# Attention with the keys on the partitions: row maximum from a separate pass, probabilities never transposed

## The reference, cut to what matters

```python
q = (x @ wq).reshape(B, S, 8, 64)      # S = 1250 tokens, 8 heads of 64
k = (x @ wk).reshape(B, S, n_kv, 64)   # repeated to 8 heads
v = (x @ wv).reshape(B, S, n_kv, 64)
scores = einsum('bhqd,bhkd->bhqk', q, k) / sqrt(64)
attn = softmax(scores, axis=-1)        # over the 1250 keys
out = einsum('bhqk,bhkd->bhqd', attn, v)
x = x + out.reshape(B, S, 512) @ wo
```

## Time and profile before

| | |
|---|---|
| median of 3 runs | 1988.69 us (1987.15 to 1989.66) |
| the profiled execution, span from first to last instruction | 1983.8 us |
| PE busy | 1641.4 us, 83% of the span, 7770 matmul instructions |
| PE weight loads busy | 1121.7 us |
| DVE, ACT, POOL busy | 798.2, 506.5, 391.0 us |
| chain that ended last | PE 58%, DMA 15%, DVE 13%, ACT 6% |

### The profile page before, as it was taken

One profiled execution on the slowest core, in us unless ns is written; L12 is line 12 of the kernel. 1 busy time (PEld: TensorE's weight loads), 2 busy tenths in 40 slices (PEclk: granted clock), 3 DMA queues, 4 the chain that ended last, 5 costly groups with the idle time before them and its releaser, 6 DMA issues.

```text
span 1983.8 us, 19802 instructions
## 1 busy us (share of the span) xinstructions
PE 1641.4 (83%) x7770; PEld 1121.7 (57%) x7770; DVE 798.2 (40%) x1511; ACT 506.5 (26%) x734; POOL 391.0 (20%) x248
## 2 busy tenths in 40 slices
PE   1999979989998849888888887899888751999895
PEld 1547645456555638677777763465765641656452
DVE  5021051399502652477777863360334224111100
ACT  1101102012301032477777751100214110101000
POOL 3100021020201120244444423200211002222112
PEclk9999999989998969899999998999998855999997
DMA  4000010100020010101000003000200452699993
GB/s 169 0 0 1 0 44 0 58 1 1 41 86 0 6 64 33 46 14 27 14 13 14 22 8 142 5 22 0 85 0 1 177 224 98 266 406 402 404 418 129
DMA packets 23236, 170.74 MB, mean 86 GB/s; under 512 B 4259, under 2 KB 4805, under 8 KB 16886
## 3 DMA queue, kind: packets, MB, share of 16 engines
q1 hardware_dynamic: 19568, 164.44, 21.0%
q0 software_dynamic: 3584, 5.12, 1.2%
HBM read 153.06 MB, written 16.49 MB: 85 GB/s over the span
## 4 chain that ended last, share of the span: by engine, by line
PE 58%; DMA 15%; DVE 13%; ACT 6%; issue 4%; POOL 2%; another core or an unknown queue 1%; SPq 0%; DVEq 0%; POOLq 0%; ACTq 0%
PE psum L839 15%; DMA out_x<-arena,idx 12%; PE psum L849 9%; PE psum L866 6%; PE psum L980 6%; PE psum L1065 4%; PE psum L858 4%; PE psum L1053 3%; DVE arena_r L1449 3%; PE psum L1035 2%; DMA xf_dram<-arena 2%; DVE neg_max L1428 2%; ACT arena_r L762 1%; DVE ln_st L1219 1%; DVE arena L1227 1%
## 5 line engine op out<-in xcount | busy, mean ns | idle before, releaser
L839 PE MATMUL psum<-arena 125*128 125x512 f32 (+3 forms) x864 | 306.5, 516 | 14.4 <-DMA arena<-in_w_in 11.6
L839 PEld LDWEIGHTS psum<-arena 125*128 125x128 f32 (+1 forms) x864 | 164.1, 190 | 156.2 <-issue 142.2
L866 PE MATMUL psum<-arena 128*125 128x512 f32 (+3 forms) x464 | 162.6, 509 | 17.1 <-DVE arena L1556 9.0
L541 POOL TENSOR_SCALAR arena<-arena,row_inv 125x1250 f32<-125x1250 f32 x40 | 138.4, 3459 | 192.3 <-DVE row_inv L1436 192.3
L1200 PE MATMUL psum<-arena 128*39 128x512 f32 (+1 forms) x704 | 159.1, 609 | 13.2 <-DMA arena<-in_w_down 10.2
L1053 PE MATMUL psum<-ident,arena 125*125 125x125 f32 x800 | 125.6, 283 | 49.8 <-DVE arena_r L1449 48.5
L1449 DVE TENSOR_TENSOR arena_r<-psum,arena_r 125x500 fp32r<-125x500 f32 x200 | 131.9, 672 | 42.1 <-ACT arena_r L762 32.3
L1053 PEld LDWEIGHTS psum<-ident,arena 125*125 125x125 f32 x800 | 102.9, 188 | 63.0 <-DVE arena_r L1449 58.3
L762 ACT ACTIVATE arena_r<-psum 125x500 fp32r<-125x500 f32 x200 | 114.3, 586 | 88.0 <-PE psum L1053 87.8
L866 PEld LDWEIGHTS psum<-arena 128*125 128x125 f32 (+2 forms) x464 | 81.2, 191 | 95.2 <-issue 71.4
L980 PE MATMUL psum<-arena 125*125 125x512 bf16 (+1 forms) x588 | 119.8, 359 | 12.8 <-DVE arena L1340 11.3
(11 more groups left out here) (279 smaller groups left out, 2051.4 us busy)
## 6 DMA issues: line engine op xcount, KB each, us to landing
arena<-in_w_down SPq DMA_DIRECT2D x32, 2816.0 KB, 23.5
arena<-in_w_up SPq DMA_DIRECT2D x32, 682.5 KB, 19.4
a_spill<-arena SPq DMA_DIRECT2D x1, 6103.5 KB
arena<-a_spill SPq DMA_DIRECT2D x1, 6103.5 KB
bc<-k_dram SPq DMA_DIRECT2D x16, 312.5 KB, 4.2
gw<-in_gw SPq DMA_DIRECT2D x2, 2048.0 KB, 10.6
arena<-in_wkqv SPq DMA_DIRECT2D x1, 3072.0 KB, 16.4
arena<-in_x SPq DMA_DIRECT2D x10, 250.0 KB
```

What stands on the lines that cost most here:

```text
L541: pool.tensor_scalar(PR[i], PR[i], row_inv[:, i:i + 1], None, ALU.mult).then_inc(p_even, 1)
L839: ins = pe.matmul(o[0:w, lo:hi], lhs(c, m), rhs(c)[:, lo:hi], start=c == 0, stop=c == k - 1)
L866: ins = pe.matmul(o[0:p, 0:w], lhs(c, t), rhs(c, t), start=c == 0, stop=c == k - 1)
```

## The change

K is projected before Q. For each head, PE first makes the whole 1250 x 1250 score matrix from the high parts alone, 64 rows deep, queries on the partitions, one tile of 125 queries at a time (`max_scores`, one PSUM region); DVE takes the negated row maximum of each tile. Ten matmuls with one stationary column each turn the ten columns of maxima into one row (`turn_max`), which ACT copies to row 64 of `QM`, below the high queries that a DMA copies there.

Then the scores are made again with the keys on the partitions. A step is one tile of 125 keys by 420 queries; a round is 10 steps, a head 3 rounds (`ROUNDS`, queries 0 to 420, 416 to 836, 830 to 1250), so 240 steps in all. `score_tile` sums two fp32r matmuls: high keys against high and low queries (128 rows), low keys and a row of ones against high queries and the row of negated maxima (65 rows). ACT writes the exponential to a ring of 6 tiles. `weigh_values` multiplies it by V in fp32, columns 0 to 210 to PSUM partitions 0 to 63, columns 210 to 420 to partitions 64 to 127. DVE adds the even tiles of a round, POOL the odd ones, and `key_sums` sums over the partitions with a stationary of ones (64 columns); DVE inverts and multiplies. The transposes, the parts of the probabilities, the scaling by the inverse and the parts of V are gone. The next head's 10 tiles of maxima are put into steps 0, 2, 5, 7, ... 22 of a head, its `turn_max` after step 25.

```diff
+QW, QH = 420, 210
+ROUNDS = [(0, QW), (416, 416 + QW), (N - QW, N)]
+STEPS = len(ROUNDS) * TILES
+MAX_STEPS = {0: 0, 2: 1, 5: 2, 7: 3, 10: 4, 12: 5, 15: 6, 17: 7, 20: 8, 22: 9}
+P_RING = 6
+        max_bank = psum[0:TOK, 0:1536]
+        mrow_bank = psum[0:1, 0:TILES * 128].rearrange("p (t n) -> p t n", n=128)
+        av_bank = [psum[:, 1536 + 512 * i:1536 + 512 * i + QH] for i in range(2)]
+        sum_bank = psum[:, 2560:2560 + QH]
+        st_bank = [psum[0:TOK, 3072 + 512 * i:3072 + 512 * i + QW] for i in range(2)]
...
 # SP, for each head h, after the two loads of KD
+                sp.wait_ge(q_hi, h + 1)
+                if h:
+                    sp.wait_ge(st_full, STEPS * (h - 1) + 1)
+                load("qm", QM[h % 2][0:DK].bitcast(F32), QS[64 * (h % 2):64 * (h % 2) + 64, h].bitcast(F32))
...
 # POOL
+                pool.tensor_tensor(KLO[h % 2][0:DK], KD[0:DK], KHH[h % 3][0:DK].bitcast(F32),
+                                   ALU.subtract).then_inc(k_split, 1)
...
+            for s in range(HEADS * STEPS):
...
+                elif t % 2 and t > 3:
+                    pool.wait_ge(p_ready, s + 1)
+                    pool.wait_ge(pool_added, adds_done(s) - 1)
+                    pool.tensor_tensor(SUM_POOL[rnd % 2], SUM_POOL[rnd % 2], PT[s % P_RING], ALU.add).then_inc(pool_added, 1)
+                if at == 4 and h + 1 < HEADS:
+                    split_keys(h + 1)
...
 # ACT
+            def max_row(h):
+                act.wait_ge(mrow_full, h + 1)
...
+                act.activation(row.rearrange("p (t n) -> p t n", n=TOK), mrow_bank[:, :, 0:TOK], ACT.Copy).then_inc(mrow_ready, 1)
+            for s in range(HEADS * STEPS):
+                h, at = divmod(s, STEPS)
+                act.wait_ge(st_full, s + 1)
+                if s >= P_RING:
+                    act.wait_ge(av_step, s - P_RING + 1)
+                    act.wait_ge((dve_added, pool_added)[(s - P_RING) % TILES % 2], adds_done(s - P_RING))
+                act.activation(PT[s % P_RING], st_bank[s % 2], ACT.Exp).then_inc(p_ready, 1)
+                if at == 12 and h + 2 < HEADS:
+                    key_highs(h + 2)
+                if at == 26 and h + 1 < HEADS:
+                    max_row(h + 1)
...
 # PE
+            def max_scores(h, t):
...
+                else:
+                    pe.wait_ge(max_ready, i)
+                for lo, hi in CHUNKS:
+                    ins = pe.matmul(max_bank[:, lo:hi], QS[own, h, tok(t)], KHH[h % 3][own, lo:hi], start=True, stop=True)
+                ins.then_inc(max_full, 1)
+            def score_tile(s):
...
+                if s >= 2:
+                    pe.wait_ge(p_ready, s - 1)
+                pe.matmul(o, KHH[h % 3][:, tok(t)], QS[:, h, q0:q1], start=True, stop=False)
+                pe.matmul(o, KLO[h % 2][:, tok(t)], QM[h % 2][:, q0:q1], start=False, stop=True).then_inc(st_full, 1)
+            def weigh_values(s):
...
+                pe.wait_ge(p_ready, s + 1)
+                for j in range(2):
+                    ins = pe.matmul(av_bank[rnd % 2][64 * j:64 * j + 64], VA[:, t, h * DK:h * DK + DK],
+                                    PT[s % P_RING][:, j * QH:j * QH + QH], start=t == 0, stop=t == TILES - 1)
+                ins.then_inc(av_step, 1)
+            def key_sums(rnd):
...
+                for i, sums in enumerate((SUM_DVE, SUM_POOL)):
+                    for j in range(2):
+                        ins = pe.matmul(sum_bank[64 * j:64 * j + 64], ones_dk[:], sums[rnd % 2][:, j * QH:j * QH + QH],
+                                        start=i == 0, stop=i == 1)
             for t in range(TILES):
                 split_row(ROW["ffn_v"] + t, t, XLT_PARTS, WV_PARTS)
+                if t < 7:
+                    max_scores(0, t)
+                elif t < TILES - 1:
+                    max_scores(0, t) if t == 7 else None
+                    max_scores(0, t + 1)
+            turn_max(0)
...
+            for s in range(HEADS * STEPS):
+                h, at = divmod(s, STEPS)
+                if s + 2 < HEADS * STEPS:
+                    score_tile(s + 2)
+                weigh_values(s)
+                if s % TILES == 3 and s >= TILES:
+                    key_sums(s // TILES - 1)
+                if h + 1 < HEADS:
+                    if at in MAX_STEPS:
+                        max_scores(h + 1, MAX_STEPS[at])
+                    if at == 25:
+                        turn_max(h + 1)
...
 # DVE
+            def normalise_heads(rnd):
...
+                dve.reciprocal(sum_inv[:], sum_bank).then_inc(sum_inverted, 1)
...
+                for j in range(2):
+                    half = slice(64 * j, 64 * j + 64)
+                    dve.tensor_tensor(ATT[own, h // 2, q0 + j * QH:q0 + j * QH + QH], av_bank[rnd % 2][half], sum_inv[half],
+                                      ALU.mult).then_inc(att_ready, 1)
+            for s in range(HEADS * STEPS):
...
+                elif t % 2 == 0 and t > 2:
...
+                    dve.tensor_tensor(SUM_DVE[rnd % 2], SUM_DVE[rnd % 2], PT[s % P_RING], ALU.add).then_inc(dve_added, 1)
+                if h + 1 < HEADS and at in MAX_STEPS:
+                    bound(h + 1, MAX_STEPS[at])
+                if t == 5 and rnd:
+                    normalise_heads(rnd - 1)
```

More of the change, by code:

```diff
@@ L228, in build @@
         KD = bc[:, 0:N]
[L229 to L235, removed]
+        KHH = [part_r(8, C * D, N), part_r(8, C * D + N, N), part_r(4, 0, N)]
+        KLO = [part_r(3, i * N, N, DK + 1) for i in range(2)]
+        QM = [part_r(3, (2 + i) * N, N, DK + 1) for i in range(2)]
+        VA = rows(7)
+        PT = [part(1, i * QW, QW, TOK) for i in range(P_RING)]
+        SUM_DVE = [part(1, (P_RING + i) * QW, QW, TOK) for i in range(2)]
+        SUM_POOL = [part(1, (P_RING + 2 + i) * QW, QW, TOK) for i in range(2)]
+        ATT = cols(2)
+        max_bank = psum[0:TOK, 0:1536]
[3 more added lines that the diff above has]
+        st_bank = [psum[0:TOK, 3072 + 512 * i:3072 + 512 * i + QW] for i in range(2)]
         XN2, XN2T = rows(1), cols(2)
@@ L708, in _, with key_highs @@
                 act.activation(XLT_PARTS[0][:, c], XLT[:, c], ACT.Copy).then_inc(xl_hi, 1)
+            act.wait_ge(loads["wk"], 16)
+            act.activation(WK_PARTS[0], WK, ACT.Copy).then_inc(proj_hi, 1)
             act.wait_ge(loads["wq"], 16)
             act.activation(WQ_PARTS[0], WQ, ACT.Copy).then_inc(proj_hi, 1)
-            act.wait_ge(loads["wk"], 16)
-            act.activation(WK_PARTS[0], WK, ACT.Copy).then_inc(proj_hi, 1)
+            drain_cols("ffn_k", 4, lambda m: KF[:, m])
+            act.wait_ge(loads["wv"], 16)
+            act.activation(WV_PARTS[0], WV, ACT.Copy).then_inc(proj_hi, 1)
+            def key_highs(h):
+                act.wait_ge(loads["kd"], 32 * (h + 1))
+                if h >= 3:
+                    act.wait_ge(st_full, STEPS * (h - 2))
+                act.activation(KHH[h % 3], KD, ACT.Copy).then_inc(k_hi, 1)
             for m in range(4):
@@ L745, in scale_odd @@
[L745 to L770 removed]
+                    act.wait_ge(st_full, STEPS * (h - 1))
@@ new lines, in max_row @@
+                row = QM[h % 2][DK:DK + 1]
+                act.activation(row.rearrange("p (t n) -> p t n", n=TOK), mrow_bank[:, :, 0:TOK], ACT.Copy).then_inc(mrow_ready, 1)
+            max_row(0)
+            act.wait_ge(rows_full, ROW["ffn_v"] + TILES)
+            key_highs(1)
+            for s in range(HEADS * STEPS):
[9 more added lines that the diff above has]
+                    max_row(h + 1)
@@ new lines, in turn_max @@
+            def turn_max(h):
+                pe.wait_ge(max_ready, TILES * (h + 1))
+                for t in range(TILES):
+                    ins = pe.matmul(mrow_bank[:, t, 0:126],
+                                    neg_max[:, TILES * (h % 2) + t:TILES * (h % 2) + t + 1], ident_r[:], start=True, stop=True)
+                ins.then_inc(mrow_full, 1)
+            def score_tile(s):
+                h, at = divmod(s, STEPS)
+                rnd, t = divmod(at, TILES)
+                q0, q1 = ROUNDS[rnd]
+                o = st_bank[s % 2]
+                if at == 0:
+                    pe.wait_ge(k_split, h + 1)
+                    pe.wait_ge(loads["qm"], 16 * (h + 1))
+                    pe.wait_ge(mrow_ready, h + 1)
+                if s >= 2:
+                    pe.wait_ge(p_ready, s - 1)
+                pe.matmul(o, KHH[h % 3][:, tok(t)], QS[:, h, q0:q1], start=True, stop=False)
+                pe.matmul(o, KLO[h % 2][:, tok(t)], QM[h % 2][:, q0:q1], start=False, stop=True).then_inc(st_full, 1)
@@ L1466, in _ @@
+            normalise_heads(HEADS * len(ROUNDS) - 1)
             for g, (lo, hi) in enumerate(GROUPS):
```

244 lines of the change are left out of this document (96 added, 148 removed), and 2 rows, old and new, of the table loads.

## The result

| | median us | range, runs | ratio to before |
|---|---|---|---|
| before | 1988.21 | 1987.15 to 1989.66 | |
| changed | 2009.48 | 1998.34 to 2015.26, 4 runs | 1.0098 [1.0064, 1.0132] |

The change makes the kernel slower by about 1%. I had forecast 1985.5 us, with 0.38 on slower and a range to 2022; the likeliest case was wrong. The profiled execution is the fastest of the four (1998.34 us, span 1996.5), 12.7 us longer than the one of before.

The account below looks back on a forecast made before the run. PE bounds, each change of array shape paid: the stage sums 45.6 + 1 + 7 x 44.9 + 34.4 + 3.2 = 398.5, taken as 395 against 398.2; 1980.6 span plus 4.9 gives 1985.5 us, range 1925 to 2022.

Parts of the forecast that it names:

- Prices on PE: Attention on PE: matmul prices per column and instruction, giving a 1.12 us step and 44.9 us per head.
- the stall: Near each head's end, PE stands 0.8 us behind ACT's copy of the row of maxima and the next exponential.
- Rival B: Value products: the two column halves don't overlap in a group of four; 42 us more, 2028 us; chance 0.10.
- 3.5 us off the stage: Tiles of maxima: half of 7 us taken off in case their 64-row loads come close together, giving 395.
- The change of shape: PE in every step: each change of array shape costs 0.093 us, plus the first load bare.
- Rival A: Attention steps: changing shape costs little, DVE binds at 36.4 us per head; about 70 us less, 1915; chance 0.20.
- DVE, ACT, POOL beside PE: Attention: the other engines stay off the path; per head ACT 20.5, DVE 28.3, POOL 16.3 of 44.9 us.
- rival C: Attention: DVE or POOL late, or ACT behind its key copy; 16 to 24 us more, 2002 to 2010; chance 0.20.
- The start: From V's projection to the first exponential: V ends at 828.0, first exponential at 833.4; 45.6 us plus 1 for the clock.
- then key_highs(1) 1.24: Before the first exponential: ACT's copy of head 1's high keys costs 1.24 us after the row of maxima.
- step 12: Within a head: ACT's high-key copy falls behind a tile of maxima, and its DMA has 8 steps to land.
- PE idles 3 us there and the clock may fall as it does now: Before the first exponential: PE idles 3 us, and a fall of the clock costs 1 us.

Follow-up runs that it names:

- e8: e5 with ScalarE's copy of the next head's row of maxima moved behind exponential 27 of a head: 1939.11 us, ratio 0.9745.
- e1: Changed kernel with head 1's keys loaded ahead of the output weights: 1996.92 us, ratio 1.0039.
- e0: The changed kernel once more, only the loads of the edge counters given bounds: 2010.17 us, ratio 1.0114.
- e2: Changed kernel, load order kept, with 36 useless 512-column matmuls after the first two score tiles: 1990.59 us, ratio 1.0011.
- e6: e1 with 6, 7 and 10 useless matmuls where PE waits around the first steps: 1983.64 us, ratio 0.997.
- e3: e1 with ScalarE held by 24 chained copies ahead of exponential 95, in head 3: 2022.01 us, one run.
- e10: Kernel before the change, with ScalarE held by 30 copies at unit 16 of the attention (head 3): 1997.47 us, one run.
- e4: e6 with values and key sums on the whole array, and the normalisation at tile 7 of a round instead of 5: 2078.39 us, ratio 1.0433.
- e7: e4 with ScalarE held ahead of exponential 95 in head 3, as in e3: 2088.46 us, one run.
- e9: e4 with the normalisation back at tile 5: 2019.97 us, ratio 1.0158.
- e5: e6 with two score tiles, then two value products per turn: 1960.88 us; ratio 0.984 from the four runs of 1950 to 1961 us.

## Why the prediction was wrong, by its own steps

**Prices on PE: right, a little high.** Step 1.12, measured 1.09; maxima 0.76 and 0.76; key sums 0.71 and 0.71; the stall 0.8 and 0.90. The step alone makes a head 30 x 0.03 = 0.9 us shorter than forecast. Rival B was out: the values of a step hold PE for 0.51 us, where I had 0.553 and three slots would have made it 0.73. One term was wrong: I took 3.5 us off the stage in case the loads for 64 rows cost little, but a tile of maxima has the full 0.76.

**The change of shape: right.** I had 0.093 for a change and the first load bare on top, 0.197 in all for a load of the whole array and 0.199 for two of 64 columns. e8 measures the two together as 0.36, which is 0.18 each; how much of it is the wait and how much the bare load wasn't taken apart. Rival A was out. The rule of the Trainium skill that I set beside it ("TensorEngine Tiling (Array Packing)", Key Properties: a change of mode drains the engine) agrees with this trace, with e8's 0.38 against 0.19 for the first and the later score matmul.

**DVE, ACT, POOL beside PE: right.** The exponential takes 521 ns, within 510 to 600; the maxima 1459 (1449), the inverse of 210 columns 1460 (1.46 us). One price was open, and rival C stood on it: an addition on DVE while POOL adds. It exists. Timeline of DVE and POOL after:

```profile
944.50 1.08 POOL L580 TENSOR_TENSOR arena<-arena 125x420 f32<-125x420 f32 x1 [3.86 <-ACT arena L797]
944.71 1.33 DVE L1530 TENSOR_TENSOR arena<-arena 125x420 f32<-125x420 f32 x1
```

DVE's addition is recorded at 1.33 us and ends 0.46 after POOL's. In e8 two additions meet the other way round:

```profile
1008.32 0.59 DVE L1544 TENSOR_TENSOR arena<-arena 125x420 f32<-125x420 f32 x1
1008.53 1.31 POOL L584 TENSOR_TENSOR arena<-arena 125x420 f32<-125x420 f32 x1 [0.37 <-ACT arena L797]
```

DVE is first, takes 0.59, and POOL's grows from 1.08 to 1.31. That agrees with the Trainium skill ("SBUF — State Buffer", section "SBUF: two separate sides"): two such instructions exclude each other for their whole length. It raised DVE to 32.6 us of a head where I had 28.3, and cost the time nothing: PE waits for no DVE in heads 1 to 7. Rival C's number, 2002 to 2010, holds the result; its mechanism didn't occur, in no row.

**The start: the step that failed.** Two terms of it. The forecast's sum, before the 3.5 us came off, is divided here where the trace is: head 1's first score tile is due two steps (2.24 us) before head 1's own part begins.

| part of the stage, us | forecast | measured | |
|---|---|---|---|
| V's first matmul to the first step | 45.6 | 53.4 | +7.8 |
| from there to head 1's first score tile | 43.7 | 56.3 | +12.6 |
| heads 1 to 6 | 269.4 | 262.4 | -7.0 |
| head 7 to the output projection | 39.8 | 39.4 | -0.4 |
| sum | 398.5 | 411.5 | +13.0 |

The first is "then key_highs(1) 1.24". I gave it its own length and not its DMA, and the measured wait for that DMA is 6.26 us. The change moves K ahead of Q, and the loads on SP keep their places behind the wait for V's last tile; of every step that is moved past a queue, what stands behind it there has to be listed, and I listed it for step 12 only. e1, which moves one load, brings the first row from 53.4 to 47.2; its second row is still 55.6, since the clock stays low.

The second is "PE idles 3 us there and the clock may fall as it does now [...]: 1 us". I took the price from the old stream. The new one stays at half clock for 41 us, and 68 in e0, whose time is nearer the median. e2, in which only the idle is filled, is 19.6 us under e0; e6, with both faults mended, has 47.3 and 40.7 us in the two rows. e3 and e10 show that the difference lies in the stream and not in the place: 54.6 us low with a wait of 6.52 us, 10.2 us with one of 8.57.

The median is 24.0 us above the forecast. Of these 16.5 are the stage (411.5 against 395) and 8.1 are the median's distance from the span of the profiled execution (13.0 us, where I had 4.9), which e0's longer low stretch fits; outside the stage it is 0.6 us less.

What in the new stream keeps the clock down isn't settled. In e4 and e7, whose values fill the array, waits of 2.2 and 5.61 us were followed by 10.2 us low at most, which points to the matmuls in column halves. (e9 says nothing on this: it has no low stretch, and no wait in its heads is over 0.7 us.) That PE is full isn't enough by itself: in e7's second low stretch it was busy for all of the 10.2 us, and the clock came back. But e4 differs also in its waits and in its length of matmuls, and e5, with half of the changes of shape, was low for 34.1 us twice. So it isn't the number of changes by itself.

Without both faults (e6) the time is 1983.6, near the forecast of 1985.5, but that is partly luck. The stage is 389.9 where I had 395: heads of 43.7 us instead of 44.9. In that execution 1593.0 us lie outside the stage and before the change 1585.6, so most of the stage's 8.3 us don't show in the span. Below the median of before it is 4.7 us; what lies outside the attention wasn't followed.

## What to carry to other kernels

List for the first iteration of a loop what each queue has ahead of the load that it needs; a sum made from the steady state says nothing of it. Where PE has a dense stream of short matmuls in column halves, a wait of 1.4 to 2 us can cost some 15 us more through the clock (head 0 of e1 against e6, 58.6 and 43.8; the long heads of e5), and one of 6 us or more some 20 (e2, e3). Useless matmuls in the gap, or, in e8, a copy put one place later on ScalarE, take it back. Look at how the work is grouped by the shape of the array: two steps at a time instead of one, with that copy moved, was worth more here (2.3% from e6 to e8, by their ratios) than the whole change of algorithm with its start mended (0.3%).

## What the hardware showed that I had not expected

- Half clock for 34.1, 41, 54.6 and 68 us at a stretch while PE was 87 to 100% busy (e1, after, e3, e0), against 10.2 us in the old stream, where PE stood for more than half of it (e10).
- The stretch isn't the same for the same wait: after 1.4 us in e5 it was 34.1 us twice, 3.4 us twice, and did not come in three heads. After waits of 1.0 us or less in the heads (after, e6, e8, e9) it never came.
- A value product on the whole array and one in column halves make the same step, 1.09 us, though one streams 0.35 us more: the two changes of shape cost what the halves save.
